# Softmax attention: values of two units visited together behind the second, in TensorE's merged order

## The reference, cut to what matters

```python
xq, xk = apply_rotary_emb(xq), apply_rotary_emb(xk)
xk, xv = jnp.repeat(xk, N_REP, axis=2), jnp.repeat(xv, N_REP, axis=2)
scores = jnp.einsum('bqhd,bkhd->bhqk', xq, xk) / math.sqrt(HEAD_DIM)
scores = jnp.where(causal[None, None], scores, -jnp.inf)
probs = jax.nn.softmax(scores.astype(jnp.float32), axis=-1).astype(xq.dtype)
out = jnp.einsum('bhqk,bkhd->bqhd', probs, xv).reshape(b, s, N_HEADS * HEAD_DIM)
return out @ Wo
```

## Time and profile before

| | |
|---|---|
| time, median of 3 runs | 3075.8 us (3075.79 to 3076.62) |
| time of the profiled execution | 3073.0 us |
| its span | 3071.3 us |
| scores of the attention's units, first to last exponential | 155.1 to 641.5 us |
| busy share of the span | TensorE 96%, VectorE 52%, ScalarE 47%, POOL 45% |
| mean granted TensorE clock | 0.982 of full speed |

### The profile page before, as it was taken

One profiled execution on the slowest core, in us unless ns is written; L12 is line 12 of the kernel. 1 busy time (PEld: TensorE's weight loads), 2 busy tenths in 40 slices (PEclk: granted clock), 3 DMA queues, 4 the chain that ended last, 5 costly groups with the idle time before them and its releaser, 6 DMA issues. The chain is left out here.

```text
span 3071.3 us, 54286 instructions
## 1 busy us (share of the span) xinstructions
PE 2943.8 (96%) x18200; PEld 2347.3 (76%) x18200; DVE 1584.1 (52%) x2732; ACT 1447.3 (47%) x2519; POOL 1393.0 (45%) x1228
## 2 busy tenths in 40 slices
PE   7799999989999999999999999999999999999958
PEld 6444444357888888888888888888888888888857
DVE  6677777737544444433444446433444444344468
ACT  5266666644444444444444444444444444444432
POOL 5411111132545555555555554555555555545530
PEclk9799999999999999999999999999999999999979
DMA  4411212001111111111111121111111111111121
GB/s 144 120 27 28 40 28 40 15 32 68 44 44 38 45 44 38 44 48 44 38 44 44 38 66 66 44 48 44 38 44 44 38 43 49 45 38 44 44 99 56
DMA packets 102575, 149.39 MB, mean 49 GB/s; under 512 B 24213, under 2 KB 44437, under 8 KB 102234
## 3 DMA queue, kind: packets, MB, share of 16 engines
q1 hardware_dynamic: 102490, 148.26, 16.4%
HBM read 129.48 MB, written 18.35 MB: 48 GB/s over the span
## 5 line engine op out<-in xcount | busy, mean ns | idle before, releaser
L1860 PE MATMUL bank<-l_xC,l_w_T 128*128 128x512 f32 x2304 | 561.9, 393 | 0.0
L1860 PEld LDWEIGHTS bank<-l_xC,l_w_T 128*128 128x128 f32 x2304 | 427.9, 188 | 88.0
L1860 PE MATMUL bank<-l_xT,l_w_T 128*128 128x512 f32 x1728 | 453.0, 400 | 6.5 <-DVE l_gT L1739 6.4
L789 DVE TENSOR_REDUCE att_max<-bank 128x1 f32<-128x640 f32 (+6 forms) x352 | 354.9, 1028 | 106.2 <-PE bank L829 102.3
L752 ACT ACTIVATE att_exp<-bank 128x512 f32<-128x512 f32 x576 | 323.5, 596 | 148.7 <-PE bank L844 142.5
L1739 DVE TENSOR_TENSOR l_kT<-bank,l_qT 128x512 f32<-128x512 f32 x128 | 88.6, 692 | 569.4 <-PE bank L1860 569.4
L1822 PE MATMUL bank<-l_v_T,l_xT 128*128 128x256 f32 x3072 | 376.9, 285 | 5.3 <-PEq L1013 2.7
L1822 PEld LDWEIGHTS bank<-l_v_T,l_xT 128*128 128x128 f32 x3072 | 375.6, 190 | 7.9 <-issue 5.6
L1860 PEld LDWEIGHTS bank<-l_xT,l_w_T 128*128 128x128 f32 x1728 | 310.3, 188 | 69.7 <-DVE l_gT L1739 12.6
L1875 PE MATMUL bank<-l_o_T,l_y_hi 128*128 128x512 f32 x1024 | 326.3, 393 | 2.5 <-DVE l_acc L1786 2.5
L1552 POOL TENSOR_TENSOR l_qd<-l_qT,l_q_decay 128x1024 f32<-128x1024 f32 x64 | 151.9, 2374 | 371.9 <-ACT l_qT L1636 371.9
(11 more groups left out here) (279 smaller groups left out, 5035.8 us busy)
## 6 DMA issues: line engine op xcount, KB each, us to landing
l_w_raw<-in_L_attn_qkv_w SPq DMA_DIRECT2D x196, 256.0 KB, 2.8
l_w_raw<-in_L_attn_gate_w SPq DMA_DIRECT2D x66, 256.0 KB, 2.7
l_o_raw<-in_L_attn_out_w SPq DMA_DIRECT2D x33, 512.0 KB, 3.6
query_parts<-att_exp SPq DMA_DIRECT2D x48, 128.0 KB
att_QT<-query_parts SPq DMA_DIRECT2D x16, 384.0 KB, 5.5
X<-x_rows SPq DMA_DIRECT2D x3, 2048.0 KB, 13.7
X<-in_L_attn_x SPq DMA_DIRECT2D x4, 1024.0 KB, 10.8
att_QT<-query_parts SPq DMA_DIRECT2D x16, 256.0 KB, 5.4
```

The source lines that it names most:

```text
L789: dve.tensor_reduce(mx[:, g % 2, heads[0]:heads[-1] + 1, q], columns(slot, q, len(heads), step), AX_X, ALU.max).then_inc(s_read, 1)
L1860: mm = pe.matmul(ps_p[p_bank(event)][:, :], w[:, SLOT[pair], LEFT[i], P * c:P * c + P], quarter(i, x, xc, c), start=(n == 0 and i in (1, 6 ...
```

## The change

The values of units 2m and 2m + 1 are both placed at 2m + 3.625. For the odd unit that is its old place, for the even unit one later. The list is sorted by position and keeps the order of equal ones, so the two stand side by side. Where a half ends with an even unit, its copy, and for half 1 the turning back, also go one later.

```diff
-        placed += [(U + 1 + VALUES_LAG, 2, ("values", U)) for U in range(ALL)]
+        placed += [(U // 2 * 2 + 2 + VALUES_LAG, 2, ("values", U)) for U in range(ALL)]
         for G in range(GROUPS):
-            summed = [NU * G + HALF_DONE[half] + 1 + VALUES_LAG for half in range(2)]
+            summed = [(NU * G + HALF_DONE[half]) // 2 * 2 + 2 + VALUES_LAG for half in range(2)]
             placed += [(summed[half] + 1.1, 3, ("keep", G, half)) for half in range(2)]
             placed.append((summed[1] + 1.6, 4, ("back", G)))
```

## The result

The changed kernel takes 3087.27 us (median of 7 runs, 3086.48 to 3089.49) against 3075.80 us (7 runs, 3073.36 to 3077.49): 11.5 us slower, a ratio of 1.0042 over all runs with a 95% interval of 1.0033 to 1.0051 (the two medians alone give 1.0037). The forecast was 3085.3, slower.

The account below looks back on a forecast made before the run. TensorE was taken to set the pace, with only two banks for each emptying engine to work ahead in. 8.6 us up to unit 132 plus 0.9 behind gave +9.5 on 3075.8: 3085.3 us, range 3073 to 3096.

Parts of the forecast that it names:

- What bounds, and the direction: Softmax attention: TensorE sets the pace, busy 30.11 of 30.81 us per group; the changed kernel was forecast slower.
- the four rules: TensorE's waits: exponentials start 0.42 after scores; scores need banks 0.05 after exponentials; reduces start 0.2 after rounds; rounds follow reduces by 0.06.
- The gain: At each of 72 pairs of values, two changes of mode go: 0.19 us saved each, 13.7 us in all.
- The waits: Between double visits, TensorE's waits for exponentials and reduces grow by 2.9 us per 18 units, a net loss of 1.2.
- no DMA is moved past another: On SP: it waits for the same scores and maxima as before, so the order of DMAs stays.
- kept sums: ScalarE's copies of finished sums are in time, some 3 us ahead of the values that overwrite their bank.
- the ring: Ring of five exponentials: no wait, since the values five units back stay at least 1.4 units ahead.
- Up to unit 132: Units 3 to 132, where the maxima end: 7.2 times 1.19 us lost, that is 8.6 us.
- Behind it: After the maxima end, scores and values alone: 5.93 against 5.76 us, 0.17 for each of five pairs, 0.9 us.
- Only the changes of mode go: Rival for the double visits: ScalarE and VectorE get far enough ahead, waits don't grow, 13.7 us stay: 3062; chance 0.08.
- A boundary shows its load: Rival inside a pair: the second unit's four weight loads wait for the first unit, 6 us less gain: 3091; chance 0.06.
- The two nearly cancel: Rival on the sum: waits grow by a quarter to 0.87 of the forecast, time near 3079; chance 0.26.

Follow-up runs that it names:

- both cuts: Reduces cut to 32 columns per head, exponentials after the first five units to 64 of 512, in paired and unpaired kernels: 3013.09 paired against 3023.22 unpaired.
- The filler: Paired kernel plus one 512-column matmul ahead of each score's wait, from score 2 of unit 132 to unit 138: 3090.11 us, ratio 1.0050 to the kernel before.

## Why the prediction was right

The direction and the mechanism up to unit 131 were right. That the time came within 2.0 us is in part luck: two errors of opposite sign stood against each other, as shown below.

*What bounds, and the direction.* Right. TensorE sets the pace, and the order decides through the four rules; the rows of after repeat them (M4 0.06 behind its reduce, 0.63 idle where 0.62 was worked out).

*The gain.* Its mechanism was right, its size low: "0.19 to 0.20 saved" was 0.24. Way in and way out cost 0.10 each, as read. The rest is that only the first pass of a visit takes 0.45, and I took 0.45 for all: the passes behind it, over the boundary between two units too, take 0.43. The rule of the Trainium skill ("TensorE: Matmul & The Clock Gate", "The mechanism") by which the second unit's weights would have to wait did not show here: the second unit's loads ran while the first unit streamed (402.98 to 403.11), and with both cuts eight pairs in nine were shorter by 0.24. The same section also lets a load run ahead into a background weight buffer, which the prediction left out; no run here shows which way these loads took.

*The waits.* "Waits grow by 2.9": 3.2 by the lengths (1.06 lost and nine times 0.24 given back). The pairs one by one: 7.87, 7.30, 6.87, 6.73, 7.81, 6.29, 7.00, 6.67, 6.28 were forecast; 7.83, 7.12, 6.89, 6.70, 7.67, 6.25, 6.99, 7.09, 6.15 came. Before they were 7.80, 7.09, 6.30, 6.62, 7.70, 6.22, 7.04, 6.51, 6.35, so the third and the eighth carry the loss (0.59 and 0.58), and in the other seven gain and waits cancel. The eighth is the one that failed, by 0.42; the sum of the nine came out right only because the other eight were 0.55 shorter than forecast. The step that failed there: "no DMA is moved past another" is true, but the score that waits for a DMA moved nearer to it. I had taken the waits for kept sums and for the ring through the new order, and not the wait for the maxima's rows.

*Up to unit 132.* "8.6 us": 6.6 for the kernel with only these pairs, by medians; 7.5 in the profile (438.92 us from the end of V(3) to score 3 of unit 131, before 431.39). The mean granted clock of that kernel's runs was 0.0004 higher than before, which is some 1 us.

*Behind it.* "0.9 us" was the term that failed: 6.0 alone. The waits are as forecast where the clock is up (0.13 against 0.17 a pair); what I left out is the clock, where TensorE waits 1.7 us for the last turn and then, without V(130), only makes scores with gaps between them until the double visit. How much of the 6 us is the clock is settled only roughly. In the profile after, the three stretches with a fall lose 5.37, of which 3 x 0.13 are waits as in the other two; the rest, 5.0, is about the most that the fall can explain: by the mean clocks TensorE was at half for 2 x (0.26 x 9.89 + 0.14 x 6.41 + 0.21 x 8.06) = 10.3 us, which can have cost 5.1 at most. Over the runs of the kernel with only these pairs the estimate was 3.7 at most. What the fall depends on stays open. The filler held the clock up in one place and not in the other, with unpaired values it fell once too, and the same 1.7 us without a matmul stands in the profile of before, at full clock:

```profile
607.95 0.23 PE L883 MATMUL bank<-identity_bf,att_max_part 128*96 128x128 bf16 x1 [1.71 <-DVE att_max_part L777]
```

*The rivals.* "Only the changes of mode go" needs engines that don't hold TensorE up: that is the kernel with both cuts, where pairing gains 10.1 us. "A boundary shows its load" is excluded: it asked for 0.53 between the passes, and 0.42 came. "The two nearly cancel" is what happens in seven pairs of nine, but not in the sum. (A slip in its working: with 0.87 of the growth the sum of the prediction gives +6.8; +6.2 needs 0.84. Nothing hangs on it.) In all, +9.5 stood against a measured +11.5: one term was 2.0 too high and the other 5.1 too low, against two parts that come to 12.6 by themselves.

## What to carry to other kernels

A visit of TensorE to another mode costs its way in and out, and it is at the same time the cover under which the other engines empty its banks: with two banks, as here, it covers two results, so a visit twice as long covered no more, and the stretch without one has to be paid. Before a step is moved in a merged order, walk through every semaphore between the places, DMA landings among them, since the instructions left behind come nearer to each other. And if such a walk shows small waits everywhere, the order itself is worth more than the change: here two scores before each visit and two before the rounds, with the turn one round later, gave 22 us.

## What the runs showed of the hardware that was not expected

- Behind the first pass of a visit, column-tiled float32 matmuls of 512 columns follow each other in 0.42 to 0.43 us, over a change of weights as within a unit; only the first pass takes 0.45 to 0.46. The loads of the next unit's weights (0.13 us for four) ran under the pass before.
- The granted clock left 2.4 GHz for 1.2 behind the last maxima (mean 0.74 in the stretch that holds 1.7 us without a matmul and goes on with scores and gaps of some 0.5). The same idle time, followed by one score and a visit, did not bring it down in the profile of before (1.00), but in one profile with the same order of values there it did, too (0.72 in 606 to 612). At half clock a double visit took 3.58 us in place of 1.86.
- With the reduces cut to 32 columns a head and the exponentials to an eighth, TensorE's busy time in 18 units equals their length (56.88 us both). A modelled busy time hides small waits, but the prediction's own walk gives 55.1 + 1.7 = 56.8 us of work, so next to nothing waits any more, and about 4.75 us of the 61.63 were waits.
- From SP's row for the turned maxima to the score that waits for them 2.76 to 3.13 us passed at this place in the profiles of the paired kernels (3.13 in the one with the filler).
